# A decoder with three kinds of expert layers on one core: shared experts as three one-pass products, more of them before and after the routed pairs

## What is computed

```
E, K, F = (64, 4, 128)          # routed experts, choices per token, hidden size
S, SF = (2, 128 * 4)            # shared experts, hidden size
CAP = 64                        # tokens kept per expert
logits = flat @ router_w.T
scores = softmax(logits); _, topk_idx = top_k(logits + router_bias, K)
topk_w = scores[topk_idx] / sum
...                             # position of each choice in its expert; those past CAP dropped
xg = flat[tok_table]
y = down(silu(gate(xg)) * up(xg))
out = zeros.at[tok_table].add(y * w_table)
sg = einsum('nd,sfd->nsf', flat, sh_gate_w); su = einsum('nd,sfd->nsf', flat, sh_up_w)
out = out + einsum('nsf,sdf->nd', silu(sg) * su, sh_down_w)
```

## Time and profile before

| | us |
|---|---|
| median of 3 runs | 2406.82 (2404.61 to 2408.33) |
| the profiled execution's own time | 2391.43 |
| its span, first to last instruction | 2389.7 |
| PE busy | 2143.7 (90%) |
| DVE busy | 1359.8 (57%) |
| ACT busy | 799.1 (33%) |
| POOL busy | 676.3 (28%) |

### The profile page before, as it was taken

One profiled execution on the slowest core, in us unless ns is written; L12 is line 12 of the kernel. 1 busy time (PEld: TensorE's weight loads), 2 busy tenths in 40 slices (PEclk: granted clock), 3 DMA queues, 4 the chain that ended last, 5 costly groups with the idle time before them and its releaser, 6 DMA issues. The chain is left out here.

```text
span 2389.7 us, 30995 instructions
## 1 busy us (share of the span) xinstructions
PE 2143.7 (90%) x10708; PEld 1141.6 (48%) x10711; DVE 1359.8 (57%) x3183; ACT 799.1 (33%) x1325; POOL 676.3 (28%) x944
## 2 busy tenths in 40 slices
PE   9999979979999999889999987478888888879994
PEld 5777748754444444344444443233333333336762
DVE  5866768856112217376667674945656555455443
ACT  5554624420122211233434332523323232123333
POOL 1200015526323320333343333011113121223543
PEclk9999989989999999999999998689999999999997
DMA  7211232270277753543333420300000000075555
GB/s 266 75 36 53 88 128 75 94 289 1 85 233 247 244 164 145 141 98 88 81 85 78 94 54 1 114 3 1 2 19 2 19 28 19 18 210 129 100 98 168
DMA packets 101672, 231.31 MB, mean 97 GB/s; under 512 B 18886, under 2 KB 42614, under 8 KB 94366
## 3 DMA queue, kind: packets, MB, share of 16 engines
q1 hardware_dynamic: 78974, 187.64, 25.3%
q0 software_dynamic: 22560, 41.87, 8.0%
HBM read 170.49 MB, written 63.53 MB: 98 GB/s over the span
## 5 line engine op out<-in xcount | busy, mean ns | idle before, releaser
L2083 DVE CUSTOM_DVE_ANT_0 D_ps<-D_ps,D_mask 128x256 f32<-128x256 f32 (+1 forms) x512 | 186.6, 418 | 69.3 <-PE D_ps L1980 68.0
L1832 POOL TENSOR_SCALAR_AFFINE_SELECT D_probs<-D_probs 128x256 f32<-128x256 f32 x256 | 106.3, 421 | 287.1 <-ACT D_probs L1890 286.8
L1890 ACT ACTIVATE D_probs<-D_ps 128x512 f32<-128x512 f32 (+1 forms) x256 | 125.3, 542 | 164.9 <-PE D_ps L2002 164.9
L3082 DVE TENSOR_REDUCE F_neg_max<-F_ps 128x4 f32<-128x2048 f32 (+1 forms) x64 | 93.9, 1488 | 107.9 <-PE F_ps L2980 101.8
L2832 ACT ACTIVATE F_probs<-F_ps 128x1536 f32<-128x1536 f32 (+1 forms) x48 | 76.4, 1591 | 186.0 <-PE F_ps L2996 186.0
L1393 PE MATMUL C_ps<-C_down_shared,C_hs 128*128 128x512 f32 x256 | 115.4, 600 | 2.1 <-DVE C_hs L1560 2.1
L1381 PE MATMUL C_ps<-C_xT,C_gate_shared 128*128 128x512 f32 x256 | 115.4, 593 | 0.7 <-DMA C_up_shared<-moe_sh_up_dram 0.7
L1381 PE MATMUL C_ps<-C_xT,C_up_shared 128*128 128x512 f32 x256 | 115.1, 592 | 0.0
L1980 PE MATMUL D_ps<-D_k_stack,D_q_stack 96*128 96x256 bf16 (+1 forms) x512 | 93.6, 269 | 8.6 <-DVE D_maxima L2083 7.1
L1230 POOL DMA_INDIRECT expert_sums<-C_y,C_of_slot x32 | 50.2, 1570 | 173.7 <-ACT C_y L1297 95.1
L2713 POOL TENSOR_SCALAR_AFFINE_SELECT F_probs<-F_probs 128x512 f32<-128x512 f32 x64 | 41.1, 653 | 177.8 <-ACT F_probs L2832 177.8
(11 more groups left out here) (549 smaller groups left out, 4877.6 us busy)
## 6 DMA issues: line engine op xcount, KB each, us to landing
C_ring<-moe_experts_dram SPq DMA_DIRECT2D x32, 1536.0 KB, 7.1
qk_parts<-D_parts SPq DMA_DIRECT2D x32, 384.0 KB, 2.5
expert_sums<-A_zeros SPq DMA_DIRECT2D x1, 8192.0 KB, 27.8
C_ring<-expert_sums SPq DMA_DIRECT2D x5, 1536.0 KB, 10.0
D_q_stack<-qk_parts SPq DMA_DIRECT2D x16, 384.0 KB, 4.9
D_k_stack<-qk_parts SPq DMA_DIRECT2D x16, 384.0 KB, 7.9
B_w<-ctxT_dram SPq DMA_DIRECT2D x1, 4096.0 KB, 16.2
B_c<-ctx_dram SPq DMA_DIRECT2D x4, 1024.0 KB, 7.1
```

What stands on the lines that cost most here:

```text
L1832: last = nc.gpsimd.affine_select(now[:, :, 0:P], now[:, :, 0:P], [[0, 2], [1, P]], ALU.is_ge, 0.0, base=0, channel_multiplier=-1)
L1890: nc.scalar.activation(probs[at % 2][:, 2 * pair:2 * pair + 2, 0:w], ps[:, 4 + unit % 3, :].rearrange("p (h q) -> p h q", h=2)[:, :, 0:w], ...
L2083: last = nc.vector.tensor_tensor_reduce(now, now, mask[:, first:256], 1.0, -3e38, ALU.add, ALU.max, maxima[n % 2][:, head, t:t + 1])
L3082: last = nc.vector.tensor_reduce(neg_max[n % 2][:, :, t], ps[:, 0:GROUP, at:at + w], AX_X, ALU.max, negate=True)
```

## The change

Shared experts: each product is made of three fp32r matmuls instead of one fp32 matmul. ACT copies the high part of gate, up and down weights, of x (per unit) and of hs (per step); DVE subtracts it from the full value to get the low part; PE multiplies high by high, high by low and low by high. Low parts of the weights lie where the weights were. To find room only one shared expert's weights are in SBUF at a time: units 0 to 3 use the first, 4 to 7 the second, which SP loads among the pairs; the ring has three buffers, and a pair's weights come in two loads (gates' part, down part), each with a semaphore of its own. 24 steps are early, 16 in the middle, 24 late. The routing's DVE work is in five pieces (`pick`, `choices` and `choose`, `weigh`, `place_choices`, `share_out`) between the steps, and batches 2 and 3 stand further back. In the late steps the sums and moments are spread over more steps. In the last layer the token list is turned two matmuls before the end of the last gate product, DVE's copies stand ahead of the last hidden step, and the first two turns stand between the down products.

```diff
-EARLY_STEPS = 20
-LATE_UNITS = 2
-RING = 4
+EARLY_STEPS = 24
+LATE_UNITS = 3
+RING = 3
...
+                if q == pair_at(LAST_GATE) + 1 + RING:
+                    sp.wait_ge(up_s, HALF)
+                    load_gates(0, 1)
+                    load_gates(1, 1)
...
+                    sp.wait_ge(gated, q - RING + 1)
+                    load_pair_gates(q)
...
+                    sp.wait_ge(y_in_psum, q - 2 - RING + 1)
+                    load_pair_down(q - 2)
...
+            def high_hs(m):
+                act.wait_ge(hs_ready, m + 1)
+                nc.scalar.copy(hs_hi[:, m % KF, :], hs[:, m % KF, :]).then_inc(hs_hi_ready, 1)
...
+                        for k in range(KD):
+                            nc.tensor.matmul(ps[:, bank + part, :], w_hi[part][:, k, now], x_hi[:, k, :], start=(k == 0), stop=False)
+                        pe.wait_ge(x_lo_ready, unit + 1)
+                        for k in range(KD):
+                            nc.tensor.matmul(ps[:, bank + part, :], w_hi[part][:, k, now], x_lo[:, k, :], start=False, stop=False)
+                        pe.wait_ge(w_lo_ready[part], half * KF + i + 1)
+                        for k in range(KD):
+                            last = nc.tensor.matmul(ps[:, bank + part, :], w_lo[part][:, k, now], x_hi[:, k, :], start=False, stop=(k == KD - 1))
...
+            def low_hs(m):
+                dve.wait_ge(hs_hi_ready, m + 1)
+                nc.vector.tensor_tensor(hs_lo[:, m % KF, :], hs[:, m % KF, :], hs_hi[:, m % KF, :].bitcast(F32), ALU.subtract
+                                        ).then_inc(hs_lo_ready, 1)
...
             pick(0)
+            choices(0)
             choose(0)
+            low_of_gates(0, 0, 0)
+            low_x(0)
+            low_of_gates(1, 0, 0)
+            low_of_gates(0, 0, 1)
+            low_of_gates(1, 0, 1)
             pick(1)
...
+                            if (u, m, bank, k) == (1, MF - 1, m, KD - 2):
+                                turn_who()
...
+                    if u and t in (0, 1):
+                        turn_x(0, t)
```

More of the change, by code:

```diff
@@ L1103, in sb, with sb_at @@
             return ctx.enter_context(nc.sbuf_tensor("C_" + name, shape, dt))
+        def sb_at(place, name, shape, dt):
+            return nc.alloc_sbuf_tensor_at("C_" + name, shape, dt, offset=place).ap()
         def sem(name):
@@ L1274, in shared_gate @@
                     nc.scalar.activation(th_s[m % 2][:], ps[:, bank, :], ACT.Tanh, scale=0.5).then_inc(th_s_ready, 1)
+                    if side_by_side(n) and i:
+                        high_hs(m - 1)
+                    if not side_by_side(n) or i == KF - 1:
+                        high_hs(m)
+                elif i == 0 and unit + 1 < UNITS:
+                    high_x(unit + 1)
+                if n == LAST_GATE + 2:
+                    high_of_gates(0, 1)
+                if n == LAST_GATE + 3:
+                    high_of_gates(1, 1)
+                if n == LAST_DOWN + 3:
+                    high_of_down(1)
             def turned(q):
@@ L1366, in shared_step @@
                 unit, down, i = step_of(n)
-                g, s = divmod(unit, SHARED)
+                half = unit // B
                 if not down:
@@ L1385, in shared_step @@
                     c = unit * KF + i
-                    if n == KF:
-                        pe.wait_ge(down_in, 16)
+                    now = slice(i * P, (i + 1) * P)
+                    pe.wait_ge(down_hi_ready, half + 1)
                     if c >= 2:
@@ L1391, in shared_step @@
                     for m in range(KF):
-                        pe.wait_ge(hs_ready, unit * KF + (m + 1 if i == 0 else KF))
-                        last = nc.tensor.matmul(ps[:, 2 + c % 2, :], hs[:, m, i * P:(i + 1) * P],
-                                                down_shared[:, s * KF + m, :], start=(m == 0), stop=(m == KF - 1))
+                        pe.wait_ge(hs_hi_ready, unit * KF + (m + 1 if i == 0 else KF))
+                        nc.tensor.matmul(ps[:, 2 + c % 2, :], hs_hi[:, m, now], down_hi[:, m, :], start=(m == 0), stop=False)
+                        pe.wait_ge(down_lo_ready, half * KF + m + 1)
+                        nc.tensor.matmul(ps[:, 2 + c % 2, :], hs_hi[:, m, now], down_lo[:, m, :], start=False, stop=False)
+                        pe.wait_ge(hs_lo_ready, unit * KF + (m + 1 if i == 0 else KF))
+                        last = nc.tensor.matmul(ps[:, 2 + c % 2, :], hs_lo[:, m, now], down_hi[:, m, :], start=False, stop=(m == KF - 1))
                     last.then_inc(down_s, 1)
@@ L1494, in pick, with choices @@
                 steps.after(last)
-            def choose(b):
+            def choices(b):
                 steps.after(nc.vector.tensor_copy(at[:], best_at[:, :, 0:K_C].rearrange("p t k -> p k t")))
@@ L1561, in shared_step @@
                     dve.wait_ge(hs_ready, m + 1)
+                    if not side_by_side(n):
+                        low_hs(m)
                 else:
                     c = unit * KF + i
-                    row = acc[:, unit // SHARED * GROUP + i, :]
+                    row = acc[:, unit % B * GROUP + i, :]
                     dve.wait_ge(down_s, c + 1)
@@ L1568, in shared_step @@
                     dve.wait_ge(added, c + 1)
+                    if i == 1 and unit + 1 < UNITS:
+                        low_x(unit + 1)
+                if n in (LAST_GATE + 2, LAST_GATE + 3):
+                    for m in range(KF):
+                        low_of_gates(n - LAST_GATE - 2, 1, m)
+                if n == LAST_DOWN + 3:
+                    for m in range(KF):
+                        low_of_down(1, m)
             def hidden(q):
@@ L3686, in _ @@
             keep_xT(0, 0)
+            low_of_weights(5)
             keep_xT(0, 1)
-            low_of_weights(5)
             low_x(0, 0)
```

259 lines of the change are left out of this document (186 added, 73 removed).

## The result

| | before | after |
|---|---|---|
| median of 14 runs each | 2405.4 us | 2414.3 us |
| ratio | | 1.0043, 95% interval 1.003 to 1.0055 |
| the profiled execution's time, span | 2391.4, 2389.7 | 2414.4, 2411.6 |
| PE's mean granted clock in it | 0.959 | 0.940 |

The change makes the kernel some 9 to 10 us slower; 2397 was forecast. The two profiled executions are 23 us apart, because the one of before lay 14 us under its own median. The stretches of the 64-expert layer in the changed kernel, in the columns of the earlier trace rows: early steps, pairs, the 29 add cycles, a piece of the pairs, late steps.

What follows compares the result with a forecast made beforehand. PE was taken to bound the kernel, with the chain of adds a close second limit among the pairs. Early +11.4, pairs -38.3, late +21.5 and last layer's front -4.4 gave -9.8 us: 2397 from 2406.8, range 2379 to 2414.

Steps and rivals of the forecast that it cites:

- The products: Shared experts' products on PE: a gate step falls from 6.87 to 5.54 us, a down step from 3.44 to 2.77.
- The early stretch: 64-expert layer up to the first add: late addresses starve POOL's scatters, PE idles 11 us; +11.4 us.
- The walk through DVE's order: Early steps: pricing DVE, PE and ACT work in order puts address 0 at 517.0 and address 3 at 607.3.
- The pairs: 64-expert layer, 29 add cycles: chained adds, 6.9 us for 26 cycles, 5.55 for the last three; 200.1 us, -38.3.
- the allowance for full engines: Pairs' add cycle: taken as 6.9 us, between 7.29 as now and 6.7 where the DMA engines are full.
- the second-half loads: Pairs: 3.1 MB of second-half shared weights cost half of 8 us, 4 us, the rest hidden by loads ahead.
- rival (b): Pairs: the adds gain nothing, cycle 7.5 us in 26 of 29; layer +5.8, total 2413 us; chance 0.13.
- PE's own pace: Pairs: PE would need 186 us for 16 steps and 32 pairs, 5.8 us a pair.
- Rival (a): Pairs: shorter load runs free the adds, cycle 6.4 us, 29 cycles 187 us, total 2384 us; chance 0.26.
- The late stretch: 64-expert layer after add 29: 24 steps for 16, first down step waits 5.9 us; 108 for 86.5, +21.5 us.
- The last layer's front: Last layer's start: earlier token list and gather remove PE's waits, the first tile_hid comes 4.4 us sooner; -4.4 us.
- The sum: Whole kernel: the terms give -9.8 us against the profiled 2391.4; carried over to the median of 2406.8, 2397 us.

Runs made afterwards that it cites:

- e3: The changed kernel with 24 steps among the pairs instead of 16 and 16 late instead of 24; ratio 0.9991 to the kernel before.
- e4: The changed kernel with the routing of batches 2 and 3 moved earlier on PE and DVE; ratio 0.9996 to the kernel before.
- e2: The changed kernel without the last layer's edits, so only the 64-expert layer is changed; ratio 1.0061 to the kernel before.
- e8: The changed kernel with adds of even and odd pairs going to two DRAM tables, each waiting for the last but one; ratio 0.9965 to the kernel before.
- e7: The changed kernel without the second shared expert's loads, high copies and low parts (result not whole); ratio 1.0032 to the kernel before.
- e10: The changed kernel with each pair's weights in one load of 12 KB runs, issued after its down products; ratio 1.0554 to the kernel before.
- e11: The changed kernel with a pair's two loads (4 and 2 KB runs) issued together after its down products; ratio 1.0384 to the kernel before.
- e12: The kernel before with two DRAM tables for the adds of even and odd pairs; ratio 1.0062 to the kernel before.
- e6: The changed kernel without pair loads from pair 3 on, using stale weights; ratio 0.9871 to the kernel before.
- e1: The kernel before with only the last layer's edits; ratio 0.9973 to the kernel before, 6.5 us faster.
- e5: The changed kernel with both 24 steps among the pairs (16 late) and the earlier routing; ratio 0.9939 to the kernel before, median 2382.6 us.
- e9: The changed kernel with two DRAM tables for the adds and the earlier routing; ratio 0.9915 to the kernel before, median 2381.2 us.

## Why the prediction was wrong

**The products: right.** The 24 records of a gate step run from 522.47 to 527.91, 5.44 us for 5.54. PE in order of time:

```profile
522.47 1.07 PE L1483 MATMUL C_ps<-C_x_hi,C_gate_hi 128*128 128x512 f32 x4
...
527.00 1.07 PE L1489 MATMUL C_ps<-C_x_hi,C_up_lo 128*128 128x512 f32 x4
```

**The early stretch: mechanism right, size short.** Forecast for the first scatter of batches 0, 2 and 3 and for the first gather: 517.0, 578.4, 607.3, 634.6. The profiled execution has 521.4, 583.0, 611.8, 640.1, each 4.4 to 5.5 later. The lag is there from the first. The router's 32 records took 7.06 us at a low granted clock where they took 3.76 in the trace of before; the clock of 474 to 516 us is 0.59. The change's instructions do not fix it: e3 and e4, with the same ones up to there, have 3.76 us and their first scatter at 516.4 and 516.5, and e2, which is slow there again, has 521.5. At the higher clock e3's gather is at 636.9. The walk through DVE's order was within 2.3 us; the term is about +15 in such an execution (first add at 661.0 in e8, 661.9 in e7; 665.2 in e3, whose pairs carry more steps) and was +17.2 in the profiled one, for +11.4. The 64 scatters themselves are longer too: POOL is busy with them for 67 to 71 us in the changed kernel and the experiments on it, for 62.5 to 62.8 where the layer's routing is that of before, and no run showed why. PE's idle time was 14.3 us, not 11:

```profile
643.41 1.12 PE L1514 MATMUL C_ps<-ident,C_xg 128*128 128x128 f32 x4 [14.31 <-DMA C_xg<-x,C_of_slot]
```

**The pairs: the step that failed.** The bound was named (adds one after another), and its price was wrong. "The bounds are 7.29 (as now), and 0.92 x 7.29 = 6.7, where the engines are full. I take 6.9." The 26 cycles to add 26 took (867.04 - 663.28) / 26 = 7.84 us, the last three 5.75. The forecast gained 38.3 us here, the kernel 17.4.

Neither end of the range was an end. The lower one took the engines' share for the limit, and e8 shows the limit to be the wait: one add's landing, beside a load about 7 us (e10, e11), and 0.8 us for POOL to follow. A chain of waits doesn't shorten because its engines still have room. The upper one came from five chained cycles in a row, which were cheap ones: all 15 cycles of the kernel before up to add 26 that begin 0.9 us or less behind the landing of the add before are 7.4 us on average. And those five stood where PE was the pace in any case, busy 36.46 of 36.46 us: e12, with no chain, takes 36.03 us for the same five (693.51 to 729.54).

So of the 0.94 us between 6.9 and 7.84, 0.39 is the allowance for full engines and 0.28 the second-half loads, which the forecast had priced apart at 4 us (half of 8 us at 400 GB/s, a rate that none of its rows shows; the highest there is 285): without them e7 has (858.35 - 661.85) / 26 = 7.56, and 6.2 us less over the 29 cycles. Of the last 0.27 some 0.1 is the choice of the five; the rest was not taken apart.

This is the way of rival (b), whose cycle of 7.5 gave 2413 us and a chance of 0.13. That its total lies so near the 2414.3 is in part luck: its cycle too was short, the front cost 6 us more than in its sum, and the late stretch and the last layer 3 and 2 us less.

The prediction also took 5.8 us a pair for PE's own pace; e8 and e6 have 183.6 and 182.7 us for 29 pairs, 6.3. In e8 PE stood 6.1 us of this ahead of gate products, for DVE's hid, which lies behind low parts of weights and x (2.9 us the longest, where the prediction allowed 1 us a time and called it covered by the adds' slack). In the changed kernel these 6.1 us are there as well.

**Rival (a)** is refuted by e10 and e11, not only by the total. Nor are the cycles of e7, beside 4 and 2 KB runs and without the shared loads, shorter than the chained ones beside 12 KB runs before (7.56 for 7.4).

**The late stretch: right in its mechanism, 3 us too long.** Forecast +21.5, found +18.5. The one wait in the first down step is where it was said, 3.54 us (and 0.40) for about 5:

```profile
914.01 0.79 PE L1504 MATMUL C_ps<-C_down_hi,C_hs_lo 128*128 128x512 f32 x1 [3.54 <-DVE C_hs_lo L1680]
916.06 0.79 PE L1504 MATMUL C_ps<-C_down_hi,C_hs_lo 128*128 128x512 f32 x1 [0.40 <-DVE C_hs_lo L1680]
```

What the prediction didn't ask is whether these steps had to be there. It had written that PE can't use its time among the pairs, and still counted eight more late steps as given; e3 shows that they cost nothing there.

**The last layer's front: right in its sign, its size open.** Forecast -4.4, e1 -6.5 with an interval of -2.9 to -10.3. In the profiled executions only 2 to 3 us of it can be seen between the first gates and the steady tiles. PE and POOL in e1 in order of time:

```profile
2139.90 0.25 PE L3487 MATMUL G_ps<-ident,G_whoT_f 38*128 38x38 f32 x1 [1.18 <-DVE G_whoT_f L3645]
2161.74 0.63 PE L3526 MATMUL G_ps<-ident,G_xg 128*128 128x128 f32 x4 [2.20 <-issue]
```

```profile
2141.47 0.99 POOL L3387 DMA_INDIRECT G_xg<-normed,G_who  x1 [7.32 <-DVE G_who L3651]
```

The wait of 4.28 us is gone; 1.18 for the token list and 2.20 at the third turn stand in its place.

**The sum.** With what the traces show the layer is 17.2 - 17.4 + 18.5 = +18.3 us in the profiled execution, about +14.6 by e2's median; with e1's -6.5 that is +8, and +8.9 was measured. The spans of the two profiled executions differ by 21.9: 18.3 in the layer, 4.5 between it and the last layer, -2.8 at that layer's front and 1.9 behind it. The second and the last arise where both kernels have the same instructions; e1, whose 64-expert layer is that of before, shows 4.0 of the 4.5 against the same execution.

## What to carry to other kernels

When a limit is a chain of waits, price one link as it stands beside everything that will be in flight, and don't take the engines' busy share for the floor: e8 moved more bytes per microsecond through the same queues (318 GB/s for 266) by letting two adds overlap. And read the link where it is the pace, over all its cases: five in a row in a stretch that another engine paced came out short. Before making an engine's work cheaper, find out what its time is made of where it is needed: the same change that lost 10 us here gained 13 us in e5, once the freed slack was filled with steps from another stretch and the routing was moved ahead. And a saving that uncovers a second limit and a fix for that limit are worth something only together: e12, the fix alone, was 13 us slower than the kernel before, and together with the change it is 8 us faster (e8), 17 with the earlier routing as well (e9).

## What the runs showed that was not expected

- The router's products at the head of the layer run at either clock level from one execution to the next with the same instructions before them: 32 records take 3.76 us or 7.06 (4.9 in e9 and e11, whose next 32 take 7.09), the mean granted clock of 474 to 516 us is 0.76 to 0.80 or 0.59, and the first scatter is at 516.4 or 521.4 us in e3 and the changed kernel. What decides it no run showed.
- A ring of three buffers with the load asked for one iteration ahead costs 78 to 115 us, though the DMA engines are far from busy there (0.56 in e10 between adds 0 and 29):

```profile
661.00:998.00 337.00, 212.41 (x986) 121.34 (x986) 54.59 (x131) 59.15 (x106) 71.37 (x56) 0.81 0.56 180
```

- A scatter-add of 128 rows of 2 KB lands in 4.8 us alone, about 7 beside a 1.5 MB load whatever its runs, and 7.6 in e8, where another add is in flight as well and the loads lie closer together; the two were not separated.
